# A two-layer block on one core: the same calls in a new order on all four compute engines

## The reference

```python
def _layernorm(x, axis=-1, eps=1e-05):
    m = jnp.mean(x, axis=axis, keepdims=True)
    v = jnp.var(x, axis=axis, keepdims=True)
    return (x - m) / jnp.sqrt(v + eps)
...
        A = jax.nn.sigmoid(A_param)
        A_t = A[:, None] ** t[None, :]
        K = (C_vec[:, None] * A_t * B_vec[:, None])[:, None, :]
        out = lax.conv_general_dilated(x_t, K, ...)      # causal, one filter for each channel
        out = out[..., :L] + D_vec[None, :, None] * x_t
        out = jnp.dot(jax.nn.gelu(out, approximate=False), W_proj.T) + b_proj
        return _layer_norm(x + out, gamma, beta)
...
        xr = mu_r * x + (1.0 - mu_r) * x_prev
        xk = mu_k * x + (1.0 - mu_k) * x_prev
        r = jax.nn.sigmoid(jnp.einsum('btc,dc->btd', xr, W_r))
        k_act = jnp.square(jax.nn.relu(jnp.einsum('btc,dc->btd', xk, W_k)))
        out = r * jnp.einsum('btc,dc->btd', k_act, W_v)
...
    x = x + _layernorm(_L0_attn_ref(_layernorm(x, axis=-1), ...), axis=-1)
    x = x + _layernorm(_L0_ffn_ref(_layernorm(x, axis=-1), ...), axis=-1)
```

## Time and profile before

| | |
|---|---|
| time of the runs | 151.26 us median of 3 (151.21 to 151.44) |
| span of the profiled execution, first to last instruction | 149.9 us; the page gives no other time for it, and the runs' median lies 1.3 us above |
| busy: PE, PEld | 135.8 us (91%), 116.2 us (78%) |
| busy: DVE, ACT, POOL | 131.5 us (88%), 129.7 us (87%), 132.5 us (88%) |
| DMA | 4.59 MB read from HBM, 4.19 MB written |

### The profile page before, as it was taken

How to read it: one execution, slowest core, us unless ns; L and a number is a source line. 1 busy time by engine, 2 the same in 40 slices (tenths; PEclk the granted TensorE clock), 3 DMA queues, 4 the chain that set the end, 5 groups by cost and what they waited for, 6 DMA issues and landing times.

```text
span 149.9 us, 3292 instructions
## 1 busy us (share of the span) xinstructions
PE 135.8 (91%) x950; PEld 116.2 (78%) x950; DVE 131.5 (88%) x372; ACT 129.7 (87%) x388; POOL 132.5 (88%) x211
## 2 busy tenths in 40 slices
...
GB/s 78 239 289 240 294 94 0 0 2 4 0 0 0 0 4 72 0 2 0 74 0 0 0 4 47 98 0 0 77 0 0 56 14 0 142 5 194 157 73 140
DMA packets 18705, 8.99 MB, mean 60 GB/s; under 512 B 1536, under 2 KB 18688, under 8 KB 18688
## 3 DMA queue, kind: packets, MB, share of 16 engines
...
HBM read 4.59 MB, written 4.19 MB: 59 GB/s over the span
## 4 chain that ended last, share of the span: by engine, by line
PE 70%; POOL 17%; DMA 3%; issue 2%; DVE 2%; SPq 2%; POOLq 1%
PE ps_k L863 9%; PE ps_k L864 9%; PE ps_r L875 9%; PE ps_r L874 9%; PE ps_tv L884 9%; PE ps_z L841 7%; POOL xn_pow L238 5%; PE ps_tv L854 4%; POOL x_r L229 4%; PE ps_prefix L821 4%; DMA x_all<-in_x 3%; PE ps_z L842 3%; PE ps_xT L813 3%; POOL z_r L253 2%; PE ps_prefix L827 2%
## 5 line engine op out<-in xcount | busy, mean ns | idle before, releaser
L377 ACT ACTIVATE xn<-x_all,x_bias,x_r 128x128 f32<-128x128 f32 x64 | 26.4, 494 | 0.6 <-POOL x_bias L220 0.6
L875 PE MATMUL ps_r<-mixed_T,tsT 128*128 128x128 f32 x128 | 24.7, 275 | 0.0
L874 PE MATMUL ps_r<-mixed_T,tsT 128*128 128x128 f32 x128 | 24.7, 275 | 0.0
L841 PE MATMUL ps_z<-pv_T,gelu 128*128 128x128 f32 x128 | 22.1, 275 | 0.0
L434 ACT ACTIVATE f_normal<-f,out_bias,yf_r 128x128 f32<-128x128 f32 x48 | 19.7, 492 | 1.6 <-POOL out_bias L292 1.6
L238 POOL TENSOR_TENSOR xn_pow<-xn,pow_token 128x512 f32<-128x512 f32 x16 | 20.3, 1272 | 0.0
L874 PEld LDWEIGHTS ps_r<-mixed_T,tsT 128*128 128x128 f32 x128 | 19.5, 192 | 0.5 <-issue 0.5
L841 PEld LDWEIGHTS ps_z<-pv_T,gelu 128*128 128x128 f32 x128 | 19.4, 191 | 0.5 <-issue 0.5
L397 ACT ACTIVATE junk<-ps_z 128x128 f32<-128x128 f32 x64 | 16.7, 277 | 3.2 <-PE ps_z L842 3.2
L875 PEld LDWEIGHTS ps_r<-mixed_T,tsT 128*128 128x128 f32 x128 | 19.4, 192 | 0.0
L580 DVE SCALAR_TENSOR_TENSOR ps_z<-ps_z,z_r,beta_row 128x128 f32<-128x128 f32 x64 | 17.5, 353 | 0.5 <-POOL z_r L253 0.5
(11 more groups left out here) (114 smaller groups left out, 365.7 us busy)
## 6 DMA issues: line engine op xcount, KB each, us to landing
...
w_pv<-in_W_proj ACTq DMA_DIRECT2D x1, 64.0 KB, 3.5
w_pv<-in_W_v ACTq DMA_DIRECT2D x1, 64.0 KB, 4.3
```

Source lines behind the costliest of these rows:

```text
L377: last = a_.activation(tile(xn[u % D], j), xa(u, j), ACT.Identity, bias=col(x_bias, u, j), scale=col(x_r, u, j))
L841: t_.matmul(tile(ps_z[u % 3], j), tile(gelu[u % D], j), pv_T[:, 0, :], start=True, stop=False)
L874: t_.matmul(tile(ps_r, j), tsT[u % D][:, q, l + 1:l + 1 + P], mixed_T[:, 0, :], start=True, stop=False)
L875: last = t_.matmul(tile(ps_r, j), tsT[u % D][:, q, l:l + P], mixed_T[:, 1, :], start=False, stop=True)
```

## The change

Only the four lists are written anew. Each engine has the same calls with the same numbers as before, and calls of one function keep their order among themselves; what differs is how the functions are interleaved. The functions themselves, the buffers, the semaphores and SP's list are as they were. In the changed kernel the line numbers of the functions of ACT and DVE are one lower than before, those of TensorE two lower; those of POOL are the same. A piece of the lists of ACT and POOL:

```diff
-            normalise(0); load_w_v(); copy_xT(0); normalise(1); make_mixers(); normalise(2); gelu_of(0); copy_xT(1)
+            normalise(0); copy_xT(0); load_w_v(); normalise(1); make_mixers(); normalise(2); gelu_of(0); copy_xT(1)
...
-            z_root(1, 1); y_variance(0, 1); y_root(0, 1); xn_times_pow(4); x_scale_of(5, 8, 2); y_variance(1, 1)
-            t_variance(0, 1); y_root(1, 1); xn_times_pow(5); z_variance(2, 2); t_root(0, 1); z_root(2, 2)
...
+            x_scale_of(4, 6, 2); xn_times_pow(4); z_variance(1, 1); y_variance(0, 1); z_root(1, 1); y_root(0, 1)
+            xn_times_pow(5); xn_times_pow(6); y_variance(1, 1); t_variance(0, 1); y_root(1, 1); t_root(0, 1)
+            z_variance(2, 2); z_root(2, 2); t_variance(1, 1); t_root(1, 1); scale_t_pool(1); xn_times_pow(7)
+            x_scale_of(5, 8, 2); y_variance(2, 2); y_root(2, 2); x_scale_of(6, 10, 2); xn_times_pow(8)
```

More of the change, by code:

```diff
@@ L336, in _ @@
-            t_variance(0, 1); y_root(1, 1); xn_times_pow(5); z_variance(2, 2); t_root(0, 1); z_root(2, 2)
[L337 to L355, removed]
+            x_scale_tiles(0, 0, 2); x_scale_tiles(1, 2, 4); x_scale_of(1, 1, 1); xn_times_pow(0); x_scale_of(2, 2, 2)
@@ new lines, in _ @@
+            t_variance(2, 2); t_root(2, 2); z_variance(4, 2); z_root(4, 2); scale_t_pool(3); xn_times_pow(9)
+            f_variance(0, 1); xn_times_pow(10); y_variance(4, 2); y_root(4, 2); f_root(0, 1); yf_means(0, 1)
+            out_biases(0, 1); f_variance(1, 1); f_root(1, 1); x_scale_of(7, 12, 2); t_variance(4, 2); z_variance(6, 2)
+            yf_means(1, 1); t_root(4, 2); z_root(6, 2); xn_times_pow(11); xn_times_pow(12); out_biases(1, 1)
+            y_variance(6, 2); y_root(6, 2); xn_times_pow(13); x_scale_of(8, 14, 2); scale_t_pool(5); t_variance(6, 2)
@@ new lines, in _ @@
+            z_variance(8, 2); z_root(8, 2); t_root(6, 2); f_variance(2, 2); f_root(2, 2); yf_means(2, 2)
+            y_variance(8, 2); y_root(8, 2); scale_t_pool(7); out_biases(2, 2); add_f(0); xn_times_pow(14); add_f(1)
+            t_variance(8, 2); z_variance(10, 2); f_variance(4, 2); z_root(10, 2); t_root(8, 2); add_f(2)
+            scale_t_pool(9); y_variance(10, 2); y_root(10, 2); f_root(4, 2); yf_means(4, 2); xn_times_pow(15)
+            t_variance(10, 2); z_variance(12, 2); z_root(12, 2); out_biases(4, 2); add_f(3); t_root(10, 2)
@@ new lines, in _ @@
+            y_variance(12, 2); scale_t_pool(10); f_variance(6, 2); y_root(12, 2); f_root(6, 2); scale_t_pool(11)
+            scale_fused_y_mean(); yf_means(6, 2); z_variance(14, 1); out_biases(6, 2); z_root(14, 1)
+            t_variance(12, 2); z_variance(15, 1); z_root(15, 1); t_root(12, 2); scale_t_pool(13); y_variance(14, 1)
+            f_variance(8, 2); y_root(14, 1); f_root(8, 2); add_f(4); yf_means(8, 2); out_biases(8, 2)
+            t_variance(14, 1); add_f(5); t_root(14, 1); y_variance(15, 1); y_root(15, 1); f_variance(10, 2)
```

118 lines of the change are left out of this document (58 added, 60 removed).

## The result

The changed kernel takes 152.91 us (median of 4 runs, 152.83 to 152.98), the kernel before 151.24 in the same comparison (4 runs, 151.13 to 151.44): ratio 1.0102, 95% interval 1.0085 to 1.0119. It is slower by 1.0%; 150.3 us was forecast. The profiled execution has a span of 151.0 us, 1.1 more than the profile before, and lasted 152.83. The rest of the 1.67 us lies in the profile of before: where runs of before list both numbers, the time is 1.68 to 2.02 us above the span, not 1.3, so the execution profiled first was itself some 0.4 us longer than the median. Where some executions of a kernel fell in the chip's slower state, its time and ratio are those of the others.

The account below looks back on a forecast made before the run. The prediction took TensorE, without waits from 32.88 to 142.79 us, to bound the kernel. Its terms, -1.3 + 0.4 + 0.3 - 0.4 = -1.0 us, gave 150.3 us (149.6 to 150.7), within a whole range of 149.5 to 152.1.

Parts of the forecast that it names:

- first sentence on the bound: From 32.88 to 142.79 us TensorE is busy 109.80 of 109.91 us and never waits there.
- Term 1: Start: xn_times_pow(5) comes earlier on POOL, so project(4) starts at 31.6, not 32.88: -1.3 us (-1.7 to 0).
- Term 2: Middle: new small waits of TensorE, at transpose_t(5), transpose_t(2) and project(9): +0.4 us (0 to 1.3).
- Term 3: From project(15) on: add_f(4) to add_f(7) stand among POOL's roots that ACT waits for: +0.3 us (0 to 0.9).
- Term 4: End: scale_f_late(11) moves back, gate(14) starts near 139.0, f_variance(14) some 1.6 us earlier: -0.4 us (-1.2 to +0.5).
- slower rival: If transpose_t(0) starts after about 33.3, normalise(8) starts 2.7 us late and 0.9 us reaches TensorE: 152.1 us, chance 0.20.
- "no change" rival: The early gain is eaten by waits because the four lists are so full: 151.2 us (150.9 to 151.6), chance 0.20.
- hold of subtract_y_mean: At the end, POOL's f_root(14) slows DVE's subtract_y_mean, making the end 0.5 us worse: 150.8 us, chance 0.15.

Follow-up runs that it names:

- e9: The kernel before with gates(2) to gates(9) doing only the first of two passes per tile, 7.1 us of TensorE's work left out: 150.83 us, 0.9959.
- e3: The four new lists only up to keys(0) on TensorE, then the old order, against the kernel before: 151.78 us, 1.0017.
- e17: The changed kernel with xn_times_pow(7) to (14) on POOL doing half of their work: 151.61 us, 0.9997 to the kernel before.
- e7: The changed kernel with add_f(4) to add_f(7) on POOL subtracting only the first of four tiles: 152.55 us, 1.0069 to the kernel before.
- e16: The changed kernel with POOL's calls from 115 us on reordered, t_root(12) ahead of z_root(15), add_f(4) to add_f(7) later: 156.39 us, 1.0317.

## Why the prediction was wrong, by its steps

- **Its first sentence on the bound.** "It never waits there", said of TensorE, was true but for 0.30 us, and was read as: what TensorE gains is gained. e9 shows otherwise: four engines are full together, and TensorE's lead is a lead over engines that do not come earlier.
- **Term 1**, forecast −1.3 (−1.7 to 0). project(4) came at 30.82, 2.06 earlier, of which the order gave 1.58, and prefix_sum(5) waits for convolve(4) as foreseen. The mechanism and the size were right; its worth was nothing (e3), because the term did not ask where x_scale_of(5) went. "Twelve places further down" is in front of y_root(2). W_v's later fetch was not quite free. In this execution TensorE waited for it, and the transposes of tile 1 start at 13.58 though convolve(0) was done at 13.00. Nothing of it reaches project(4): the new start takes 8.72 us from x_scale_of(4) also where W_v came in time (e3).

```profile
13.14 0.49 PE L790 MATMUL ps_k<-centre,w_pv 128*128 128x128 f32 x2 [1.07 <-DMA w_pv<-in_W_v]
```

- **Term 2**, forecast +0.4 (0 to 1.3). This is the step that failed: from −2.06 at project(4) to +0.14 at project(15) it measured 2.2. project(9) and transpose_t(2) were named, transpose_t(5) too, and lose 0.79, 0.29 and 0.11; prefix_sum(8) and project(13), 1.10 together, were not. The slack was worked out for one call, scale_t_pool(5), by counting work ahead of it (6.9 us later; it came 7.8 later, POOL's wait of 1.06 us at y_variance(6) not being in the count), and not for the roots y_root(2), z_root(6) and y_root(10), on which DVE and then project and prefix_sum hang. For these POOL is no earlier than before: 0.9 us later, as late, and 0.1 us earlier, in a profile whose start ran 0.5 us earlier. So each of these waits eats part of TensorE's lead. With POOL light (e17) prefix_sum(8), project(9) and project(13) lose 0.48 us together, not 1.89. And the sentence on the add_f calls, "moved back by up to 26 us, leave POOL's other work earlier", failed: x_scale_of and xn_times_pow took the room, and POOL waited 1.06 us at y_variance(6) besides.
- **Term 3**, forecast +0.3 (0 to 0.9), measured 1.1 (from +0.14 at project(15) to +1.25 at TensorE's end). The additions are half of it (e7). Of the rest 0.30 is transpose_t(12): z_root(15) ahead of t_root(12) there, and with the two exchanged (e16) DVE's scale_z(15) ahead of gate(10), so it takes both lists.
- **Term 4**, forecast −0.4 (−1.2 to +0.5), measured −0.2: TensorE ends 1.25 late, the span 1.1. f_variance(14) came 0.4 earlier, not 1.6. ACT, DVE and POOL at the end:

```profile
139.49 0.59 ACT L426 ACTIVATE tanh<-ps_r 128x512 f32<-128x512 f32 x1
```

```profile
139.60 0.69 DVE L609 TENSOR_TENSOR x_all<-x_all,ps_xT 128x512 f32<-128x512 f32 x1 [1.77 <-ACT ps_xT L445]
140.20 0.68 DVE L604 SCALAR_TENSOR_TENSOR f<-tanh,ps_tv 128x512 f32<-128x512 f32 x1
```

```profile
141.77 0.20 POOL L277 TENSOR_SCALAR f_ve<-yf_raw 128x4 f32<-128x4 f32 x1 [0.55 <-DVE yf_raw L513]
```

  gate(14) was to start at 139.0, when tanh_r(14) is done. It did start right behind tanh_r(14), but that was done at 140.08, 1.16 later than before: ACT comes 1.17 later to relu_k(14) already, late by terms 2 and 3. add_f_late(11), ahead of gate(14) on DVE, ends at about the same time, since scale_f_late(11) had moved back on ACT. So the term was worked out with ACT in time, as it was not.

  With these sizes the sum is −1.6 + 2.2 + 1.1 − 0.2 = +1.5 us, where the runs have +1.67.
- **The slower rival** had the right sign, about half the size (152.1) and the right pair of calls, xn_times_pow(7) and x_scale_of(5) ahead of y_root(2). But transpose_t(0) came at 32.22, before its trigger of 33.3, and ACT waited 0.29 us at normalise(8), not 2.7. The harm came all the same, since x_scale_of(5) is 2.4 us long whether it waits or not, so its sign was in part luck. The "no change" rival's mechanism, the lead eaten by waits, is what took place, with the late part on top.
- **The hold of subtract_y_mean** did not come (last section).
